# First x chunk of a two-layer FFN kernel taken in two pieces of 256 tokens, one W load moved to another queue, seven warm-up matmuls in place of ten

## The reference, cut to what matters

```python
def _L0_cond_ref(x, W_gate, W_up, W_down, A_gate, B_gate, ...):   # F = 1376, ranks of 16
    gate = lora_add(jnp.einsum('bnh,fh->bnf', x, W_gate), x, A_gate, B_gate)
    up   = lora_add(jnp.einsum('bnh,fh->bnf', x, W_up),   x, A_up,   B_up)
    act  = jax.nn.silu(gate) * up
    return lora_add(jnp.einsum('bnf,hf->bnh', act, W_down), act, A_down, B_down)
...
x = x + _L0_ffn_ref(_L0_cond_ref(x, ...), ...)      # 512x512 projection + 8 adapters
x = x + _L1_ffn_ref(_L1_cond_ref(x, ...), ...)      # masked projection, then 64 experts, top 16
```

## Time and profile before

| | |
|---|---|
| median of three runs | 361.28 us (361.18 to 361.67) |
| profiled execution, device time | 359.89 us |
| profiled execution, span from the first to the last instruction | 358.2 us |
| PE busy | 354.3 us, 99% of the span, 1728 matmul records |
| DVE / ACT / POOL busy | 197.6 / 141.2 / 83.2 us |
| DMA | 38.86 MB, mean 108 GB/s |

### The profile page before, as it was taken

The page is one execution under the profiler, slowest core; times in us unless marked ns, Lnnn a source line. Parts: engine busy times, 40 slices in busy tenths (PEclk is TensorE's granted clock), DMA queues, the critical chain, the costliest instruction groups (busy, mean ns, idle before and its releaser), DMA issues.

```text
span 358.2 us, 4760 instructions
## 1 busy us (share of the span) xinstructions
PE 354.3 (99%) x1728; PEld 299.2 (84%) x1728; DVE 197.6 (55%) x303; ACT 141.2 (39%) x191; POOL 83.2 (23%) x89
## 2 busy tenths in 40 slices
PE   8999999999999999999999999999999999999996
PEld 7888888888888888988888898888888888888886
DVE  3758664245434533576574476769888868511101
ACT  5567444234423432434662552547363353201100
POOL 1738886644240001100000000000032054002200
PEclk9999999999999999999999999999999999999999
DMA  7855542333130041579317209201042012101011
GB/s 253 274 167 168 176 133 62 113 102 88 53 108 0 0 171 47 164 276 345 96 48 214 93 2 354 116 5 53 3 158 77 2 59 73 47 29 59 31 59 59
DMA packets 14979, 38.86 MB, mean 108 GB/s; under 512 B 2305, under 2 KB 4097, under 8 KB 13681
## 3 DMA queue, kind: packets, MB, share of 16 engines
q1 hardware_dynamic: 11728, 31.24, 25.8%
q0 software_dynamic: 2656, 6.95, 6.6%
q10 hardware_dynamic: 576, 0.43, 0.4%
HBM read 36.51 MB, written 2.10 MB: 108 GB/s over the span
## 4 chain that ended last, share of the span: by engine, by line
PE 99%; DVE 0%; issue 0%
PE ps L1052 28%; PE ps L1053 28%; PE ps L1054 28%; PE ps L1174 3%; PE ps L1072 3%; PE ps L1080 1%; PE ps L1087 1%; PE ps L1103 1%; PE ps L1091 1%; PE ps L1095 1%; PE ps L1264 1%; PE ps L1251 1%; PE ps L1273 0%; PE ps L1282 0%; DVE x L1045 0%; DVE warm L746 0%
## 5 line engine op out<-in xcount | busy, mean ns | idle before, releaser
L1052 PE MATMUL ps<-x_hl,w_hl 128*128 128x512 f32 x160 | 62.8, 392 | 0.0
L1053 PE MATMUL ps<-x_hl,w_hl 128*128 128x512 f32 x160 | 62.7, 392 | 0.0
L1054 PE MATMUL ps<-x_hl,w_hl 128*128 128x512 f32 x160 | 62.3, 389 | 0.0
L383 POOL DMA_INDIRECT b_raw<-b_gu,row_of x36 | 36.1, 1003 | 34.7 <-DVE b_st L713 25.4
L421 POOL TENSOR_TENSOR am_hl<-am_raw,am_hl 128x512 fp32r<-128x512 f32 x8 | 11.1, 1392 | 136.8 <-ACT am_hl L438 136.8
L734 DVE TENSOR_TENSOR glu<-glu,ps 128x512 f32<-128x512 f32 x22 | 15.0, 685 | 37.6 <-PE ps L1072 37.6
L1054 PEld LDWEIGHTS ps<-x_hl,w_hl 128*128 128x128 f32 x160 | 30.1, 188 | 6.5
L438 ACT ACTIVATE act<-glu 128x512 f32 (+1 forms) x22 | 13.8, 632 | 54.3 <-DVE glu L734 54.2
L1052 PEld LDWEIGHTS ps<-x_hl,w_hl 128*128 128x128 f32 x160 | 30.1, 188 | 5.2
L1053 PEld LDWEIGHTS ps<-x_hl,w_hl 128*128 128x128 f32 x160 | 30.2, 189 | 4.8
L1053 PE MATMUL ps<-act,wd_hl 128*128 128x512 f32 x80 | 31.1, 389 | 0.0
(11 more groups left out here) (139 smaller groups left out, 700.6 us busy)
## 6 DMA issues: line engine op xcount, KB each, us to landing
wc_raw<-mask_w SPq DMA_DIRECT2D x8, 1024.0 KB, 7.4
w_raw<-w_gu SPq DMA_DIRECT2D x9, 512.0 KB, 3.4
wd_raw<-w_dn SPq DMA_DIRECT2D x10, 256.0 KB, 3.0
x_raw<-x_t SPq DMA_DIRECT2D x8, 256.0 KB, 5.3
w_raw<-w_t SPq DMA_DIRECT2D x2, 1024.0 KB, 6.9
x<-x_t SPq DMA_DIRECT2D x2, 1024.0 KB, 6.1
am_raw<-a_moe SPq DMA_DIRECT2D x8, 256.0 KB, 2.7
bm_raw<-b_moe SPq DMA_DIRECT2D x4, 512.0 KB, 3.8
```

What stands on the lines that cost most here:

```text
L383: nc.gpsimd.indirect_dma_start(b_raw[f % 2][:, p].rearrange("q m f -> q (m f)"), None, b_gu, bass.IndirectOffsetOnAxis(ap=row_of[:, f - 2, ...
L1052: nc.tensor.matmul(out, w_high, m_high, start=start, stop=False)
L1053: nc.tensor.matmul(out, w_high, m_low, start=False, stop=False)
L1054: return nc.tensor.matmul(out, w_low, m_high, start=False, stop=stop)
```

## The change

It has four parts. The load of the first half of x chunk 0 becomes two DMAs of 256 tokens, with a semaphore each. ACT and DVE split it in two pieces too, and TensorE multiplies it with weight tile 0 by pieces (`project_pair`), 12 matmuls of 256 columns where there were 6 of 512. Chunk 0 of weight tile 1 is loaded by SP, behind the two pieces of x, and no longer by ACT. Seven warm-up matmuls are run in place of ten. From weight tile 1's chunk 0 on, TensorE's order is what it was.

```diff
-WARM_UP = 10
+WARM_UP = 7
...
-            load_x0(0)
+            for h in range(2):
+                sp.dma_start(x_raw[:, 0, h * PAIR:h * PAIR + PAIR],
+                             x_t[:, 0, h * PAIR:h * PAIR + PAIR]).then_inc(dma_x0_pair[h], 16)
+            sp.dma_start(w_raw[1][:, 0], w_gu[1, :, 0]).then_inc(dma_w_first[1][0], 16)
             load_x0(1)
...
-            for u in range(2):
-                act_e.dma_start(w_raw[u][:, 0], w_gu[u, :, 0]).then_inc(dma_w_first[u][0], 16)
-                if u == 0:
-                    act_e.dma_start(small_sb[:], small_in).then_inc(dma_small, 16)
+            act_e.dma_start(w_raw[0][:, 0], w_gu[0, :, 0]).then_inc(dma_w_first[0][0], 16)
+            act_e.dma_start(small_sb[:], small_in).then_inc(dma_small, 16)
...
-            x_high(0, 0)
+            for h in range(2):
+                pair = slice(h * PAIR, h * PAIR + PAIR)
+                act_e.wait_ge(dma_x0_pair[h], 16)
+                copy(x_hl[:, 0, 0, pair], x_raw[:, 0, pair]).then_inc(x_hi if h else x_pair_hi, 1)
...
-            for k in range(2):
-                x_low(k, 0)
-                for u in range(2):
-                    w_first_low(u, slice(k, k + 1), 2 * k + u + 1)
+            for h in range(2):
+                pair = slice(h * PAIR, h * PAIR + PAIR)
+                dve.wait_ge(x_hi if h else x_pair_hi, 1)
+                low(x_hl[:, 1, 0, pair], x_raw[:, 0, pair], x_hl[:, 0, 0, pair]).then_inc(x_lo if h else x_pair_lo, 1)
+                w_first_low(h, slice(0, 1), h + 1)
+            x_low(1, 0)
+            for u in range(2):
+                w_first_low(u, slice(1, 2), 3 + u)
...
-            for k in range(KD):
+            def project_pair(h):
+                pair = slice(h * PAIR, h * PAIR + PAIR)
+
+                def pass_of(part_w, part_x):
+                    for m in range(2):
+                        nc.tensor.matmul(ps[:, m, pair], w_hl[0][:, part_w, 0, m], x_hl[:, part_x, 0, pair],
+                                         start=h == part_w == part_x == 0, stop=False)
+
+                pe.wait_ge(w_hi, 1)
+                pe.wait_ge(x_hi if h else x_pair_hi, 1)
+                pass_of(0, 0)
+                pe.wait_ge(x_lo if h else x_pair_lo, 1)
+                pass_of(0, 1)
+                pe.wait_ge(w_lo, 1)
+                pass_of(1, 0)
+
+            for h in range(2):
+                project_pair(h)
+            project_first(1, 0)
+            for k in range(1, KD):
                 for u in range(2):
                     project_first(u, k)
```

More of the change, by code:

```diff
@@ L189, in build @@
         warm_set = sem("warm_set")
-        dma_x0 = [sem(f"dma_x0_{k}") for k in range(KD)]
+        dma_x0 = [None] + [sem(f"dma_x0_{k}") for k in range(1, KD)]
+        dma_x0_pair = [sem(f"dma_x0_pair{h}") for h in range(2)]
+        x_pair_hi, x_pair_lo = sem("x_pair_hi"), sem("x_pair_lo")
         dma_x1 = [sem(f"dma_x1_{k}") for k in range(KD)]
```

## The result

The changed kernel took 365.01 us in the median (16 runs, 360.87 to 366.27), the kernel before beside it 361.38 (16 runs, 360.54 to 362.65). The ratio of the means is 1.0072, 95% interval 1.0043 to 1.0102: slower, clear of the noise but by under 2%. The forecast was 361.4, with 360.6 to 362.4 as its range, and "no change".

The account below looks back on a forecast made before the run. TensorE, busy 99%, was taken to bound the kernel. Lora_down +0.18 us and adapt_first −0.05 gave +0.13: 360.0 us for the profiled execution, 361.4 with the 1.39 us to the median; range 360.6 to 362.4.

Parts of the forecast that it names:

- TensorE's start: First matmul on x: from 5.38 to about 4.7 us, bounds 4.1 and 5.0; head start 0.73 us at lora_down.
- 1.43 + 0.3: First twelve matmuls of 256 columns: 1.43 us, plus 0.3 us for those at half speed before the clock rises at 5.3.
- The late clock: After the warm-ups: a hole delays the clock's rise to 8.8 us, TensorE loses 2.05 us; 362.3 us, chance 0.16.
- SP's issues: SP's queue: two more DMAs ahead of the adapter loads cost 0.94 us, moving a_raw's first issue from 7.68 to 8.62.
- ACT started the split at 13.99, 1.9 us after the last issue: a_raw's split on ACT: a_st comes 0.94 us later, at 16.81, so lora_down starts 0.18 us later.
- a gain for `b_first`: POOL's loads: small_sb landing earlier brings b_first forward; with 0.6 us of that, 360.55 us, half of a 0.14 chance.
- a wait of 0.9 us: Ahead of lora_down: the head start becomes a 0.9 us wait for a_st, and lora_down starts at about 16.87.
- `adapt_first` without a wait: At adapt_first: TensorE comes at 26.16, t_st is ready by 25.85, so a wait of 0.05 us is gone.
- The adapters aren't late: Rival at a_raw: its loads don't slip; half near 361.15 us, half near 360.55, chance 0.14.
- No earlier start: Rival at TensorE's start: weight chunk lands at 4.6, start at 5.0, the wait swallows it; 361.4 us, chance 0.08.
- The slower rival: Hole between last warm-up and first piece: clock rises at 8.8 us, costing 1.0 us net; 362.3 us, chance 0.16.
- Its sign: On PE's timeline: matmuls of 512 columns 0.43 us apart after 6 us would show the clock rising late.

Follow-up runs that it names:

- b of tile 2 early: Kernel before with one POOL wait left out, so b_raw of tile 2 is loaded right behind b_first: 360.23 us, ratio 0.9973.
- POOL waits: Changed kernel with POOL holding b_first back until SP's a_raw loads have landed: 365.71 us, ratio 1.0118.
- four by SP and x behind: Changed kernel with four a_raw loads by SP, and x chunks 2 and 3 of the second half behind them: 361.46 us, ratio 1.0001.
- opposite move: Kernel before with chunk 1 of weight tile 1 moved from SP's queue to ACT's: 361.49 us, ratio 1.0017.
- x behind: Changed kernel with x chunks 2 and 3 of the second half loaded behind SP's adapter loads: 362.36 us, ratio 1.003.
- seven warm-ups: Kernel before with seven warm-up matmuls in place of ten, all else as before: 361.28 us, ratio 1.0009.
- W on SP, x behind: Kernel before with chunk 0 of weight tile 1 on SP, and x chunk 3 of the second half behind SP's adapter loads: 361.38 us, ratio 1.0018.
- W on SP alone: Kernel before with one edit, chunk 0 of weight tile 1 loaded by SP and not by ACT: 364.26 us, ratio 1.0059.
- lateness alone: Kernel before with const_sb loaded in two pieces ahead of SP's adapter loads, two more issues in front of them: 361.03 us, ratio 0.9995.
- W back on ACT: Changed kernel with chunk 0 of weight tile 1 on ACT's queue again: 361.72 us, ratio 1.0019.
- ten warm-ups: Changed kernel with ten warm-up matmuls again, all else as changed: 363.03 us, ratio 1.006.
- filler: Changed kernel with twelve unread matmuls on zeros ahead of the wait for a_st: 362.3 us, ratio 1.003.
- six by SP: Kernel before with six a_raw loads by SP instead of five, and two by POOL: 361.84 us, ratio 1.0026.
- four by SP: Changed kernel with four of the eight a_raw loads by SP and four by POOL: 361.91 us, ratio 1.0022.
- the same with x behind and b early: Changed kernel, four a_raw loads by SP, x chunks 2 and 3 of the second half behind them, b_raw of tile 2 loaded early: 359.85 us, ratio 0.9957.

## Why the prediction was wrong, step by step

**TensorE's start: right in its sum, with two terms off that cancel.** It began at 4.25 where 4.7 was taken and 4.1 to 5.0 bounded. But the first twelve matmuls took 6.37 − 4.25 = 2.12 us where 1.43 + 0.3 was taken: the clock rose at about 5.0, and some 0.3 us went into waits for the second piece. The arrival at `lora_down` by the pace of starts is 15.9, as forecast. The late clock didn't occur in this profile. When the clock rises is not the change's doing alone: it was 5.3, 4.9, 4.4 and 6.5 us in the four profiles that have the start of before untouched (its three, and b of tile 2 early), and 4.1 to 7.0 in eight of the nine with the pieces (the ninth records none).

**SP's issues: right.** 8.68 against 8.62 for the first, 13.13 against 13.07 for the last, and plain DMAs at 0.47 each.

**The failed step: "ACT started the split at 13.99, 1.9 us after the last issue".** The prediction carried these 1.9 us over to the later issue, so that all moved by the 0.94 us of two issues (split at 13.99 + 0.94 = 14.93, `a_st` at 16.81). The split came at 17.45 and `a_st` at 19.33: 2.5 us beyond the forecast. The time from the issue of a small load to its use was taken as a constant, and it wasn't one. In the kernel before, the last issue (12.13) came 0.3 us after POOL's first of `b_first` (11.82, in the first profile); in the changed kernel 2.1 us after it (11.06). Ordered by that distance, issue to split took

| profile | last `a_raw` issue after first `b_first` issue, us | issue to split, us |
|---|---|---|
| POOL waits | -3.3 | 2.4 |
| four by SP and x behind | -0.8 | 2.4 |
| before, three profiles; b of tile 2 early | 0.3, 0.3, 1.3; 0.5 | 1.9, 1.9, 2.7; 1.6 |
| opposite move; x behind | 0.8, 1.3 | 2.6, 2.9 |
| seven warm-ups; W on SP, x behind | 1.3, 1.5 | 2.5, 2.3 |
| W on SP alone; changed kernel | 2.0, 2.1 | 4.1, 4.3 |
| lateness alone; W back on ACT | 2.3, 2.3 | 3.6, 3.8 |
| ten warm-ups; filler | 2.7, 2.8 | 4.2, 3.8 |
| six by SP | 3.7 | 4.0 |
| four by SP; the same with x behind and b early | 0.6, -0.6 | 4.4, 3.3 |

Up to 1.5 it is 1.6 to 2.9 us, from 2.0 on 3.6 to 4.3. The last row is the exception, and POOL's fourth load doesn't explain it, since SP's came last there too. So the distance isn't all. A second thing that differs is how far behind SP's own queue is: ACT was through with the x chunk ahead of `a_raw` at 11.7 us in the first profile of before, and at 13.4 with four by SP. Alone that doesn't make the adapters late either, for it was 13.4 as well with POOL held back, where the split followed 2.4 us after the issue. That the two work together is argued, not shown. The prediction named POOL's loads coming sooner as a gain for `b_first` and gave it a chance; it did not ask what they would meet. The Trainium skill, DMA: Bandwidth & Descriptors, in Queues, rings and completion order, has the rule that the prediction itself cited, that a DMA engine takes turns between the queues for which it has work, by the packet. The traces agree as far as they go: the same load took 2.4 us with POOL's held back and 3.8 to 4.3 beside them. They don't show the turns themselves. The rule was applied to `small_sb` at 2 us and not to `a_raw` at 13.

**The clock behind the hole: not in the prediction at all.** It priced a wait of 0.9 us as 0.9 us. The waits of PE between 8 and 45 us in all the profiles, and what followed: after 3.40, 3.04, 2.24, 2.13, 2.13, 2.11 and 1.80 us the granted clock fell to the lower level; after 1.93, 1.78, 1.77, 1.43, 1.07 and shorter ones it didn't. So in these profiles a wait near 2 us goes either way, and where the clock fell it cost some 1.7 us more (3.4 us at half speed) or, as in the changed kernel's profile, 2.8. That the idleness sets it off is shown by the filler, which keeps everything but that. The Trainium skill, TensorE: Matmul & The Clock Gate, in Why this matters for your kernels, advises against idle gaps of TensorE between bursts of matmuls; the traces agree, and some of the gaps after which the clock fell are shorter than those that the page names.

**`adapt_first` without a wait: not testable here**, since `lora_down` was too late. With the cures on (four by SP and x behind) it had no wait, and the head start met the b of tile 2 at 36 us, a wait that the first profile of before happened not to have.

**The rivals.** "The adapters aren't late" fell: they were later. "No earlier start" fell. The slower rival had the right sign, a loss by the clock, but in the wrong place and for another reason: it was put at the start, where the warm-ups end, and the loss came 14 us later, where the head start ended. Its sign, matmuls of 512 columns some 0.43 apart after 6 us, was seen all the same; that would be luck and not the rival's merit.

**What stays open.** Two falls in the 12 runs with six loads by SP and none with lateness alone, but 7 of 12 with the W move and 11 of 16 in the changed kernel: the move adds something to the collision. The early traffic differs: from 6 to 8 us the eight profiles with x chunk 0 whole and W's chunk 0 on ACT's queue moved 374 to 396 GB/s, the eleven with the pieces or with W on SP's queue, or both, 323 to 349. So x and W would land later, and the engines be less free when the adapters come. That this is the link is argued, not shown. And the medians of the changed kernel's two groups lie 3.7 us apart, where a mean clock of 0.995 over 361 us accounts for 1.8; later waits such as that at 34.53 would make up the rest, but only profiles show them.

## What to carry to other kernels

Work moved ahead of a wait whose end doesn't move turns into idle time of TensorE, and here idle time of 2 us was not free of charge: price it with half speed behind it, or fill it. A DMA added to a queue is not only an issue of 0.47 us: ask which other queue's large loads the small ones behind it will now meet, since the time from issue to use is no constant. And profile the kernel before more than once: here the first profile had neither the wait at 36 us, which swallowed the head start where nothing else did, nor the spread of 1.9 to 2.7 us from the last adapter load to its use.

## What the runs showed of the hardware

- One and the same program can have two times: the changed kernel took 361.7 us in the median of the runs in which the clock held and 365.4 in the median of those in which it fell.
- Twelve matmuls of 128 columns on zeros were worth 2.7 us of the median here.
- The last small load on SP's queue was in use 1.6 to 2.9 us after its issue in ten profiles, and 3.3 to 4.4 us after it in nine; holding back the indirect loads of POOL's queue took it from 3.8 to 4.3 us down to 2.4.
- With the early loads in another order the traffic from 6 to 8 us was some 13% slower, 336 GB/s in the median of eleven profiles against 387 in that of eight. The rows of before, of W's move alone, and of W back on ACT with the pieces of x kept (us, busy, clock, DMA share, GB/s):

```profile
6.00:8.00 2.00, 2.00 (x9) 1.00 1.06 396
```

```profile
6.00:8.00 2.00, 2.00 (x11) 1.00 0.94 338
```

```profile
6.00:8.00 2.00, 0.50 (x4) 1.00 0.95 326
```

Either of the two edits alone does it; why, no run here shows.
